# A two-layer graph attention kernel on one core: weight bounds, low parts and residual adds shared out between the engines, and identity transposes in the opening

## What is computed

```python
def gnn(x, adj, ...):                      # 12 heads of 32
    q, k, v = x @ Wq.T, x @ Wk.T, x @ Wv.T + bv
    scores = einsum(q, k) * 384**-0.5 + 2 * adj
    scores = where(any(scores != 0, -1), scores, -inf)
    return softmax(scores) @ v @ Wo.T + bo
def ffn(x, ...):                           # 3 experts of 128
    gate = softmax(relu(x @ Wg1 + bg1) @ Wg2 + bg2)   # top 2, softmax again
    q, k = split(x @ Wqk + bqk)            # expert 0: q through a width-3 convolution
    y[e] = causal_softmax(q_e k_e * 128**-0.5) @ (x @ Wv[e] + bv[e])
    return (y * w_e) @ Wp + bp
x = x + gnn(layernorm(x), adj)
x = x + ffn(layernorm(x))
```

## Time and profile before

| what | value |
|---|---|
| median of 3 runs | 2256.42 us (2255.87 to 2256.48) |
| the profiled execution: its time, its span | 2256.14 us, 2254.3 us |
| TensorE busy | 2200.9 us, 98% of the span |
| VectorE busy | 1916.8 us, 85% |
| ScalarE busy | 1495.3 us, 66% |
| GpSimd busy | 1115.9 us, 49% |
| opening, up to the first score of the repeated turns | 96.61 us |
| 30 repeated turns | 2045.55 us |
| ending | 112.14 us |

### The profile page before, as it was taken

The page is one execution under the profiler, slowest core; times in us unless marked ns, Lnnn a source line. Parts: engine busy times, 40 slices in busy tenths (PEclk is TensorE's granted clock), DMA queues, the critical chain, the costliest instruction groups (busy, mean ns, idle before and its releaser), DMA issues.

```text
span 2254.3 us, 51222 instructions
## 1 busy us (share of the span) xinstructions
PE 2200.9 (98%) x16905; PEld 1435.5 (64%) x16905; DVE 1916.8 (85%) x7160; ACT 1495.3 (66%) x5290; POOL 1115.9 (49%) x1351
## 2 busy tenths in 40 slices
PE   5899999999999999999999999999999999999988
PEld 2566666666666666666666666666666666666655
DVE  6988888888888888888888888888888888888894
ACT  2677666767666767666776666776666676667663
POOL 2554555454555454564444554545554545554542
PEclk9999999999999999999999999999999999999999
DMA  6221122221122221222221222211222211222200
GB/s 175 62 62 48 43 76 76 76 59 41 54 76 76 76 54 41 59 76 76 64 56 42 67 76 76 62 50 44 74 76 76 61 45 47 76 76 76 59 5 29
DMA packets 142263, 143.18 MB, mean 64 GB/s; under 512 B 16816, under 2 KB 141360, under 8 KB 142000
## 3 DMA queue, kind: packets, MB, share of 16 engines
q1 hardware_dynamic: 139808, 138.62, 23.1%
q10 hardware_dynamic: 2192, 1.29, 0.2%
HBM read 39.18 MB, written 25.17 MB: 29 GB/s over the span
## 4 chain that ended last, share of the span: by engine, by line
PE 94%; DVE 4%; issue 1%; POOL 1%; ACT 1%; DMA 0%; SPq 0%; DVEq 0%; ACTq 0%; POOLq 0%
PE B_bank L510 33%; PE A_bank L510 32%; PE A_bank L581 7%; PE A_bank L593 4%; PE B_bank L600 4%; PE A_bank L568 4%; PE B_bank L575 4%; PE B_bank L585 2%; PE B_bank L547 2%; PE A_bank L547 2%; DVE raw_score L923 1%; DVE smax L929 0%; DVE wmax L730 0%; DMA S<-in_wk 0%; POOL h L1070 0%
## 5 line engine op out<-in xcount | busy, mean ns | idle before, releaser
L683 ACT ACTIVATE S<-raw_score,smin 128x128 f32<-128x128 f32 x1536 | 593.9, 393 | 178.2 <-DVE smin L923 178.0
L1052 POOL TENSOR_TENSOR S<-S,rowf 128x512 f32<-128x512 f32 x384 | 391.9, 1048 | 353.9 <-DVE rowf L948 353.9
L923 DVE CUSTOM_DVE_ANT_0 raw_score<-A_bank,adj,s_unit 128x128 f32<-128x128 f32 x1536 | 444.5, 347 | 2.5
L1057 POOL TENSOR_TENSOR S<-S,row2f 128x384 f32<-128x384 f32 x128 | 106.0, 828 | 621.9 <-DVE row2f L956 621.6
L697 ACT ACTIVATE PT<-A_bank 128x512 f32<-128x512 f32 x384 | 220.1, 590 | 233.5 <-PE A_bank L581 233.3
L683 ACT ACTIVATION_READ_ACCUMULATOR S<-raw_score,smin 128x1 f32 x1536 | 295.9, 193 | 0.0
L581 PE MATMUL A_bank<-ident,S 128*128 128x128 f32 x1536 | 225.5, 274 | 3.3 <-DVE smin L923 1.8
L929 DVE TENSOR_REDUCE smax<-raw_score 128x12 f32<-128x1536 f32 x128 | 223.2, 1744 | 0.1
L581 PEld LDWEIGHTS A_bank<-ident,S 128*128 128x128 f32 x1536 | 186.8, 141 | 40.1 <-DVE smin L923 2.0
L690 ACT ACTIVATE S<-S,s2min 128x128 f32<-128x128 f32 x384 | 148.3, 390 | 2.0 <-DVE s2min L933 1.9
L568 PE MATMUL A_bank<-Ks,Qs 96*128 96x128 f16 x1536 | 139.3, 220 | 2.6 <-DVE smin L923 2.4
(11 more groups left out here) (182 smaller groups left out, 6118.7 us busy)
## 6 DMA issues: line engine op xcount, KB each, us to landing
xin<-in_x SPq DMA_DIRECT2D x32, 768.0 KB, 4.5
Qs<-q_hi SPq DMA_DIRECT2D x256, 96.0 KB, 2.2
out<-x1res SPq DMA_DIRECT2D x128, 192.0 KB, 2.1
Ks<-k_hi SPq DMA_DIRECT2D x252, 96.0 KB, 2.3
Qs<-q_lo SPq DMA_DIRECT2D x128, 96.0 KB, 2.2
Ks<-k_lo SPq DMA_DIRECT2D x126, 96.0 KB, 2.3
adj<-in_adj SPq DMA_DIRECT2D x32, 256.0 KB, 3.5
S<-in_wq SPq DMA_DIRECT2D x1, 576.0 KB, 5.5
```

Source lines behind the costliest of these rows:

```text
L683: ins = nc.scalar.activation(S[b % 2][:, h, :], raw_score[:, h, :], ACT.Exp, bias=smin[b % 2][:, h:h + 1], scale=-1.0, accum_out=ssum[b % ...
L923: ins = nc.vector.tensor_tensor_reduce(raw_score[:, h, :], src[:, j * T:(j + 1) * T], adj2[:, b, :], s_unit[:], 3.0e38, ALU.add, ALU.min, ...
L1052: nc.gpsimd.tensor_tensor(S[b % 2][:, hs, :], S[b % 2][:, hs, :], rowf[b % 2][:, hs].unsqueeze(2).broadcast_to([P, HPC, T]), ALU.mult).the ...
L1057: nc.gpsimd.tensor_tensor(S2[b % 2][:], S2[b % 2][:], row2f[b % 2][:].unsqueeze(2).broadcast_to([P, NE, T]), ALU.mult).then_inc(normed2, 1)
```

## The change

1. **Bounds of four weights.** wo, wp and the halves of wqk get their bound from ScalarE, as the sum of absolute values along each partition's row, and not the maximum from VectorE (`W.sum.n`). The full output of that instruction goes to the weight's low part, which is written again later. `W.turn` waits for two semaphores.
2. **Low parts of four weights.** The halves of wqk, wp and wv2 get theirs from GpSimd, in two instructions each (scale in place, subtract the high part), with a semaphore `w_lo_late`. wq, wk, wv and wo stay on VectorE.
3. **Residual adds** are four instructions of 384 columns in place of one of 1536, each with its own wait; B's adds no longer wait for the moments of all four graphs. The row of bo is loaded earlier (third in SyncE's queue behind x, ahead of wv), and adj's first scaling is a step of the table.
4. **Transposes of the identity** into a B bank that nothing reads, at six places of the opening: 12 ahead of all else, 24, 36, 18, 8 and 10.
5. `W.scale` is split: reading `top_col` is a step of its own (`W.top`).
6. **New tables** for the opening and the ending. That of the repeated turns is the old one for TensorE, ScalarE, VectorE and SyncE; on GpSimd the adds stand in four pieces at the old places.

The core of the diff:

```diff
+WARM = (24, 12, 36, 18, 8, 10)
+LATE = 4
...
     "pe": """
-        W.turn.0@0 W.spread.0@0 A.hT.0@0 A.hT.1@0 A.hT.2@0 A.qk.0@0 A.qk.1@0 A.qk.2@0 A.qk.3@0 W.turn.1@0
-        W.spread.1@0 A.qk.4@0 A.qk.5@0 W.turn.2@0 W.spread.2@0 A.v.0@0 A.v.1@0 A.score.0.0@0 A.score.0.1@0
+        W.warm.1@0 A.hT.0@0 A.hT.1@0 W.turn.0@0 A.hT.2@0 W.spread.0@0 W.warm.0@0 A.qk.0@0 A.qk.1@0 W.turn.1@0
+        A.qk.2@0 A.qk.3@0 W.spread.1@0 A.qk.4@0 A.qk.5@0 W.turn.2@0 W.spread.2@0 A.v.0@0 A.v.1@0 A.v.2@0 A.v.3@0
+        W.warm.2@0 A.score.0.0@0 A.score.0.1@0 A.hT.0@1 A.score.0.2@0 W.warm.3@0 A.score.1.0@0 A.score.1.1@0 A.score.1.2@0 W.warm.4@0 A.hT.1@1
...
+                    if kind == "warm":
+                        for _ in range(WARM[b]):
+                            nc.tensor.transpose(bank["B"][2][:, 0:P], ident[:], ident[:])
+                        return
...
-                        pe.wait_ge(maxima, (2, 6, 8)[b])
+                        pe.wait_ge(maxima, (2, 4, 4)[b])
+                        if b > 0:
+                            pe.wait_ge(sums, 2 * b)
...
+            def weight_sum(n):
+                _, (_, lo), stage, width, col = raw[n]
+                act.wait_ge(raw_loaded[n], 16)
+                nc.scalar.activation(lo[:], staged(stage, width), ACT.Abs,
+                                     accum_out=wmax[:, col:col + 1]).then_inc(sums, 1)
...
+            def split_lo(n):
+                _, (hi, lo), stage, width, col = raw[n]
+                pool.wait_ge(w_hi, n + 1)
+                nc.gpsimd.tensor_scalar(staged(stage, width), staged(stage, width), wscale[:, col:col + 1], 1.0,
+                                        ALU.mult, ALU.mult).then_inc(w_scaled, 1)
+                pool.wait_ge(w_scaled, n + 1 - LATE)
+                nc.gpsimd.tensor_tensor(lo[:], staged(stage, width), hi[:], ALU.subtract).then_inc(w_lo_late, 1)
...
                 elif kind == "res":
-                    wait_evacuated(pool, ("A", "proj", GB - 1, 0), g)
-                    pool.wait_ge(moments2, count(g, GB, GB))
+                    wait_evacuated(pool, ("A", "proj", b, 0), g)
...
-                    nc.gpsimd.tensor_tensor(x1res[:], x1[:], bp_row[:].unsqueeze(1).broadcast_to([P, GB, C]),
-                                            ALU.add).then_inc(x1res_ready, 1)
+                    nc.gpsimd.tensor_tensor(x1res[:, b, :], x1[:, b, :], bp_row[:], ALU.add).then_inc(x1res_ready, 1)
```

More of the change, by code:

```diff
@@ L110 @@
[L110 to L114, removed]
@@ L115 @@
-        A.mix.3@0 A.ln2.2@0 W.bias.0@0 A.proj.3@0 A.ln2.3@0
+        W.max.0@0 W.share.0@0 W.max.1@0 W.top.0@0 A.hT.0@0 W.scale.0@0 W.max.2@0 W.lo.0@0 A.hT.1@0 A.hT.2@0
+        W.max.7@0 W.unit.0@0 A.qk.0@0 W.lo.1@0 W.top.1@0 A.qk.1@0 A.qk.2@0 W.scale.1@0 W.lo.2@0 A.qk.3@0
+        W.top.2@0 A.qk.4@0 W.scale.2@0 A.qk.5@0 A.ln1@0 W.unit.1@0 W.values.0@0 W.lo.3@0 A.v.0@0 A.v.1@0 A.v.2@0
+        A.score.0.0@0 A.score.0.1@0 A.score.0.2@0 A.v.3@0 A.smax.0@0 A.hT.0@1 A.score.1.0@0 A.norm.0@0
+        A.score.1.1@0 A.hT.1@1 A.score.1.2@0 W.unit.2@0 A.hT.2@1 A.smax.1@0 A.norm.1@0 A.score.2.0@0 A.qk.0@1
@@ L186 @@
+        B.gate.1@0 B.score.0@0 B.score.1@0 B.turn.0@0 B.mix.0@0 B.score.2@0 B.turn.1@0 B.score.3@0 B.turn.2@0
+        B.mix.1@0 B.mix.2@0 B.turn.3@0 B.mix.3@0
     """,
     "dve": """
[L188 to L190 removed]
@@ L196 @@
-        B.score.1@0 B.norm.0@0 B.proj.3@1 B.norm.1@0 B.score.2@0 B.score.3@0 B.norm.2@0 B.mix.0@0 B.norm.3@0
-        B.mix.1@0 B.proj.0@0 B.mix.2@0 B.proj.1@0 B.mix.3@0 B.proj.2@0 B.proj.3@0
+        A.score.0.0@0 A.score.0.1@0 A.v.0@0 B.hT.0@1 A.score.0.2@0 B.hT.1@1 B.hT.2@1 A.smax.0@0 A.score.1.0@0
+        A.norm.0@0 A.score.1.1@0 B.conv@1 A.score.1.2@0 B.v.0@1 A.v.1@0 B.v.1@1 A.smax.1@0 B.v.2@1 A.score.2.0@0
+        B.v.3@1 A.norm.1@0 A.score.2.1@0 B.gate.0@1 A.score.2.2@0 A.smax.2@0 A.mix.0@0 A.score.3.0@0 A.norm.2@0
@@ new lines @@
+        A.score.3.1@0 B.gate.1@1 A.score.3.2@0 A.mix.1@0 A.proj.0@0 B.score.0@1 A.smax.3@0 A.norm.3@0 A.v.2@0
+        A.v.3@0 A.ln2.0@0 B.gate.2@1 A.mix.2@0 B.score.1@1 B.norm.0@1 A.proj.1@0 A.proj.2@0 B.norm.1@1 A.ln2.1@0
+        A.ln2.2@0 A.mix.3@0 B.score.2@1 A.proj.3@0 B.mix.0@1 B.score.3@1 A.ln2.3@0 B.mix.1@1 B.norm.2@1
+        B.proj.0@1 B.proj.1@1 B.hT.0@0 B.hT.1@0 B.hT.2@0 B.norm.3@1 B.conv@0 B.v.0@0 B.v.1@0 B.mix.2@1 B.v.2@0
+        B.mix.3@1 B.v.3@0 B.gate.0@0 A.ln1@0 B.gate.1@0 B.score.0@0 B.gate.2@0 B.score.1@0 B.norm.0@0 B.proj.2@1
@@ L455, in load_raw @@
                 sp.dma_start(staged(stage, width), src).then_inc(raw_loaded[n], 16)
-            for n in range(3):
+            for n in range(2):
                 load_raw(n)
+            sp.dma_start(rows[1][1], rows[1][0].unsqueeze(0).broadcast_to([P, C])).then_inc(bo_loaded, 16)
+            load_raw(2)
             sp.dma_start(adj2[:], dram_group(adj, 0)).then_inc(adj_loaded, 16)
@@ L738, in h_share, with weight_tops @@
                 ins.then_inc(h1_share_ready, 1)
+            def weight_tops(part):
+                n = scale_part[part].stop - scale_part[part].start
+                dve.wait_ge(maxima_turned, part + 1)
+                nc.vector.tensor_reduce(top_col[0:n, part:part + 1], bank["B"][0][0:n, 0:P], AXX,
+                                        ALU.max).then_inc(tops, 1)
             def weight_scales(part):
```

157 lines of the change are left out of this document (81 added, 76 removed).

## The result

| what | before | after |
|---|---|---|
| median | 2256.45 us (2255.87 to 2257.83, 4 runs) | 2239.03 us (2238.90 to 2239.64, 4 runs) |
| profiled span | 2254.3 us | 2236.8 us |
| opening, to the first score of the repeated turns | 96.61 us | 89.80 us |
| 30 repeated turns | 2045.55 us | 2045.18 us |
| ending | 112.14 us | 101.82 us |

What follows compares the result with a forecast made beforehand. TensorE bounds the repeated turns (idle 0.15 us), so gains lie only in 53 us of opening and ending. Opening -8.3, turns 0, ending -9.0 sum to -17.3 us from 2256.14: 2239 us, range 2230 to 2250.

Steps and rivals of the forecast that it cites:

- The ending: Stretch after the repeated turns: gate and last steps together -9.0 us, bounds -4 and -14.
- The gate's clash: Ending: GpSimd's adds stretch two VectorE gate instructions; without it TensorE's 6.81 us wait goes, 6.5 us gained (5.5 to 7.6).
- the last steps: Very end: a moved projection fills a 1.49 us wait, add pieces shorten a 2.08 us one; -2.5 us, bounds 0 and -5.
- Up to the first score: Opening until the first score's evacuation: VectorE loses maxima and waits, score at about 44.7 for 50.85, together -6.2 us.
- last k evacuation: 35.3: Opening, group 0: last k evacuation at 35.3 for 35.85, -0.6 us, bounds -2 and +2.
- wk's low part at about 26 in either case: Opening: wk's low part, needed by TensorE's qk of group 0, comes at about 26, before and after the change.
- From there to the turns: Opening, first score to repeated turns: two low parts leave VectorE before the last k evacuation, 34.5 to 31.4 us, -3.1 us.
- my first rival: Opening: GpSimd's long instructions stall VectorE's four norm row factors, up to 2.6 us each, eating the 8.3; 2247 us, chance 0.2.
- the 1.0 us that I allowed for stalls and transposes: Opening: +1.0 us for GpSimd's new instructions holding up VectorE and for the identity transposes together.
- Gain nothing, since the twelve DMAs cover them: Opening's end: three low parts leave VectorE behind the last k evacuation, no gain; stretch stays 11.25 us.
- Transposes: Opening: 108 identity transposes, 25 us if nothing hides them, let qk.0 to qk.2 run at the higher level, about 3 us shorter.
- The -0.6 us in which I booked this: Opening: earlier last k evacuation of group 0, 35.3 for 35.85, including the gain from faster matmuls behind the transposes.

Runs made afterwards that it cites:

- pieces_around: Kernel before the change, residual adds in four pieces, GpSimd's ending table laying them around the gate and behind B's first norm, other engines' tables old: 2250.70 us.
- old_ending: Changed kernel with the old table of the last steps on all engines, adds still in pieces: 2243.97 us, ratio 0.9944.
- more_transposes: Changed kernel with 18 more identity transposes, in TensorE's wait for wk's low part between qk.2 and qk.3 of group 0: 2238.00 us.
- lows_on_vector: Changed kernel with the four late low parts back on VectorE, the last three in one block behind the last k evacuations of group 1: 2244.98 us.
- no_transposes: Changed kernel without its 108 identity transposes, all else the same: 2238.98 us, ratio 0.9926.
- lows_spread: Changed kernel with the four late low parts on VectorE, each of the last three behind a projection's evacuation instead of in one block: 2245.68 us.

## Why the prediction was right, and where not

*The ending, -9.0 forecast, -10.3 measured.* The gate's clash was priced by the excess of two instructions and put at 6.5 us, as if nothing else were late. pieces_around moves GpSimd's pieces only: the wait of 6.81 us falls to 1.33, and up to group 31's first score in stage B 4.8 us are left of it, under my lower bound of 5.5. In the changed kernel that score starts 79.1 us into the ending in place of 88.7, and from there to the end it is 22.7 us in place of 23.4, with one projection of 1.5 us moved from the first part to the second. On the same work that is 8.1 and 2.2 us less. So the last steps, which I put at 2.5, were right in size, and the first part hid two errors: the gate gave less, and the new order of the other engines, to which I gave nothing of its own, some 3 us. In the last steps the waits are only in part those I named: that of 1.49 us fell by 0.75, not all of it, that of 2.08 by 1.8, not by 0.9, and one of 1.26 came in.

*Up to the first score, -6.2 forecast, -4.0 measured.* The terms from k's last evacuation to the first score held in their sum: 9.4 us forecast, 46.81 - 36.94 = 9.9. Their rows are not all tested: that the third scale comes earlier is in the order and the rows, but no run puts it back alone. The copies of k end that stretch as much as VectorE does: in old_ending, more_transposes and lows_on_vector TensorE waited 0.51, 0.73 and 0.21 us for them before the first score. The step that failed is the start, "last k evacuation: 35.3". It was 36.94, because TensorE fell to its lower level in the 2.33 us that it waited for wk's low part; where it did not, it came at 35.30 (lows_on_vector), 35.09 (more_transposes), 35.43 (no_transposes) and 34.40 (old_ending). I had said "wk's low part at about 26 in either case" and had not asked what a wait there does to the matmuls behind it. One term was right: the sum on ScalarE takes 1.16 us and 0.19 for the read of its result, 1.35 where I took 1.34. Taking the maxima off VectorE is worth 2.5 us by the run.

*From there to the turns, -3.1 forecast, -2.2 measured*, 34.5 to 32.3 us. Two low parts left, and the bias scaling, held 2.25 us by GpSimd, came in. That is my first rival, at one instruction in place of four: the row factors of the four norms took 0.17 us each. Of its excess of 2.1 us, 0.9 shows as the difference to the forecast; the 1.0 us that I allowed for stalls and transposes covers that, not the 2.1. The page "SBUF — State Buffer" of the Trainium skill, section "Who interferes with whom", counts `tensor_scalar` among the operations that can contend for the shared port pair when their operands meet the conditions of its two-port modes, besides those with two SBUF inputs: by that rule the instruction held, with one tensor input, was as much at risk as the row factors that I had watched. The trace agrees, 2.25 us against 0.16 in lows_on_vector, where no GpSimd instruction ran beside it.

*The three low parts behind the k evacuation.* "Gain nothing, since the twelve DMAs cover them": the stretch stayed nearly as long as I said, but the reason is only half. Before, the second layer's input was as late as the copies of k: the 0.15 us of idle time in the earlier trace rows, which I read as none, was TensorE waiting for that input at 100.5. Left on VectorE, they keep the other path long, in lows_spread through wp's buffer, in lows_on_vector through the norm that they hold up on GpSimd and the evacuation behind them: 6.0 and 6.7 us of the gain did not come. From k's last evacuation to the turns it is 10.7 us (79.1 to 89.80) for 11.25.

*Transposes.* I held that they make `qk.0` to `qk.2` about 3 us shorter. Those banks did become 3 us shorter than before the change, but only 1.7 of it is the transposes' (8.0 us without them, 6.3 with), and in the time it was worth nothing: the wait behind them grew, and in it the level fell. The -0.6 us in which I booked this did not come. *Repeated turns*: -0.4, for 0.

So the sum, 17.4 for 17.3, came out better than its parts: the opening's gain was put 1.5 us too high, the ending's 1.3 too low, and that they cancel is luck. Not tested by any run of its own: the earlier load of bo's row and the split of `W.scale`.

## What to carry over

A GpSimd instruction can hold up a VectorE instruction to its own end: here it did with small ones that read two SBUF inputs (2.69 and 3.14 us for 0.17) and with one scaling of three columns, and not with evacuations out of PSUM, which took their 0.69 us beside an add. The hold goes the other way too, so work left on VectorE can delay GpSimd. Cutting the long instruction in pieces bounds the hold and lets urgent work in between; moving it away whole puts its 3.4 us in front of whatever stands behind it in GpSimd's queue. Before calling work covered, look for the second path that ends at the same moment: its sign is a wait of a tenth of a us at a step that nobody thinks about. And where one stretch is shared by two parts of a change, cut the windows at the same step in every run: the medians of two kernels with the old opening, 0.7 us apart, hid 3.6 us of difference in the ending.
